# Fused attention layer: bodies of 1024 tokens, values in the score banks after the scores, and the rounding of x on ScalarE

## What is computed

```python
q = _split_heads(jnp.einsum('bfe,ed->bfd', x, W_query))
k = _split_heads(jnp.einsum('bfe,ed->bfd', x, W_key))
v = _split_heads(jnp.einsum('bfe,ed->bfd', x, W_value))
scores = jnp.einsum('hbqd,hbkd->hbqk', q, k)
attn = jax.nn.softmax(scores, axis=-1)
out = jnp.einsum('hbqk,hbkd->hbqd', attn, v)
out = out.transpose(1, 2, 0, 3).reshape(x.shape[0], x.shape[1], HEADS * ATT_D)
out = out + jnp.einsum('bfe,ed->bfd', x, W_res)
return jax.nn.relu(out)
```

## Time and profile before

| what | value |
|---|---|
| median of three runs | 1513.44 us |
| time of the profiled execution | 1513.46 us |
| its span in the trace | 1511.7 us |
| TensorE matmuls, weight loads | busy 1493.1 us, 1405.2 us |
| VectorE, ScalarE, GpSimd | busy 1390.5 us, 1044.5 us, 872.2 us |
| first scores of body 0 start at | 13.71 us |
| value product of the last body starts at | 1504.65 us |
| first projection starts at | 9.71 us |
| transpose of x on VectorE (L349), mean | 701 ns |
| POOL copies of the values (L167), mean | 467 ns |
| DMA | 67.37 MB read, 67.11 MB written, 89 GB/s |

### The profile page before, as it was taken

One profiled execution on the slowest core, in us unless ns is written; L12 is line 12 of the kernel. 1 busy time (PEld: TensorE's weight loads), 2 busy tenths in 40 slices (PEclk: granted clock), 3 DMA queues, 4 the chain that ended last, 5 costly groups with the idle time before them and its releaser, 6 DMA issues.

```text
span 1511.7 us, 77248 instructions
## 1 busy us (share of the span) xinstructions
PE 1493.1 (99%) x32768; PEld 1405.2 (93%) x32768; DVE 1390.5 (92%) x1793; ACT 1044.5 (69%) x1794; POOL 872.2 (58%) x1548
## 2 busy tenths in 40 slices
PE   7999999999999999999999999999999999999997
PEld 6999999999999999999999999999999999999997
DVE  6999999999999999999999999999999999999996
ACT  4677777777777777777777777777777777777775
POOL 3555555555555555555555555555555555555555
PEclk9999999999999999999999999999999999999999
DMA  3444444444444444444444444444444444444443
GB/s 59 98 85 96 85 96 86 96 86 95 86 96 85 96 85 96 85 96 85 96 86 96 86 96 85 96 86 95 86 96 85 96 85 96 85 96 85 96 86 77
DMA packets 677302, 135.36 MB, mean 90 GB/s; under 512 B 545888, under 2 KB 677216, under 8 KB 677216
## 3 DMA queue, kind: packets, MB, share of 16 engines
q1 hardware_dynamic: 675840, 134.30, 42.9%
q10 hardware_dynamic: 1376, 0.26, 0.1%
HBM read 67.37 MB, written 67.11 MB: 89 GB/s over the span
## 4 chain that ended last, share of the span: by engine, by line
PE 98%; issue 0%; POOL 0%; DVE 0%; ACTq 0%; DMA 0%; ACT 0%; POOLq 0%
PE ps_so L241 18%; PE ps_pt L232 17%; PE ps_so L220 14%; PE ps_qk L198 8%; PE ps_qk L196 8%; PE ps_vr L209 8%; PE ps_qk L197 8%; PE ps_vr L210 8%; PE ps_vr L211 8%; POOL y L154 0%; DMA w_raw<-in_L_rec_W_res_dram 0%; ACTq L334 0%; POOL v_diag L167 0%; DVE row_max L364 0%; ACTq L331 0%
## 5 line engine op out<-in xcount | busy, mean ns | idle before, releaser
L154 POOL TENSOR_TENSOR y<-attn,vr 128x256 f32<-128x256 f32 x512 | 387.4, 779 | 532.4 <-DVE attn L379 512.7
L167 POOL COPY v_diag<-vr 64x264 f32<-64x264 f32 x1024 | 478.7, 467 | 102.9 <-POOL y L154 39.9
L311 ACT ACTIVATE probs_t<-ps_pt 128x512 f32<-128x512 f32 x512 | 307.0, 600 | 160.2 <-PE ps_pt L232 160.1
L364 DVE TENSOR_REDUCE row_max<-ps_so 128x16 f32<-128x1024 f32 x256 | 313.5, 1225 | 69.7 <-PE ps_so L220 69.7
L298 ACT COPY vr<-ps_vr 128x512 f32<-128x512 f32 x512 | 300.6, 587 | 67.3 <-PE ps_vr L211 1.1
L196 PE MATMUL ps_qk<-x_hi,w_hi 128*128 128x256 f32 x1024 | 331.3, 323 | 10.5 <-DVE x_lo L355 9.7
L291 ACT COPY qk<-ps_qk 128x512 f32<-128x512 f32 x512 | 300.6, 587 | 56.6 <-PE ps_qk L198 9.0
L232 PE MATMUL ps_pt<-ident,shifted 128*128 128x128 f32 x2048 | 321.4, 280 | 0.8 <-ACT probs_t L311 0.8
L369 DVE TENSOR_TENSOR shifted<-ps_so,row_max 128x1024 f32<-128x1024 f32 x256 | 313.5, 1224 | 8.8
L241 PE MATMUL ps_so<-v_diag,probs_t 128*64 128x66 f32 x8192 | 296.2, 225 | 1.4 <-DVE attn L379 0.7
L198 PE MATMUL ps_qk<-x_lo,w_hi 128*128 128x256 f32 x1024 | 292.0, 285 | 0.0
(11 more groups left out here) (20 smaller groups left out, 1527.2 us busy)
## 6 DMA issues: line engine op xcount, KB each, us to landing
x_in<-in_r_x_dram SPq DMA_DIRECT2D x1024, 64.0 KB, 2.2
out_dram<-y SPq DMA_DIRECT2D x256, 256.0 KB, 2.5
w_raw<-in_L_rec_W_query_dram ACTq DMA_DIRECT2D x1, 64.0 KB, 2.2
w_raw<-in_L_rec_W_key_dram ACTq DMA_DIRECT2D x1, 64.0 KB, 2.7
w_raw<-in_L_rec_W_value_dram ACTq DMA_DIRECT2D x2, 32.0 KB, 2.7
w_raw<-in_L_rec_W_res_dram ACTq DMA_DIRECT2D x2, 32.0 KB, 2.7
```

The lines of the kernel that those rows point to most:

```text
L154: nc.gpsimd.tensor_tensor(y[:, n % 2, a * HALF:(a + 1) * HALF].rearrange("k t (p j d) -> k j (t p) d", j=2, d=D), attn[:, n % 2, a * HALF: ...
L167: nc.gpsimd.tensor_copy(v_diag[n % 2][j * F:(j + 1) * F, seq, :, :, :, j].rearrange("k a t p d -> k a (t p) d"), vr[n][seq * F:(seq + 1) * ...
L364: nc.vector.reduce_max(row_max[:, :].rearrange("q (h u) -> q h u", h=HEADS), scores, AX_X).then_inc(max_ready, 1)
```

## The change

A body becomes 8 tiles, 1024 tokens, so there are 128 bodies. A group is a pair of tiles; a body has four groups (`GROUPS`), and `upto(i, g)` counts them. What the code does differently:

- The scores of a whole body fill the four `ps_so` banks completely (8 tiles of 64 columns) in one run of 64 matmuls. When VectorE has read them, the value product of body i-1 is written into the same banks from column 0 on, in one run of 32 matmuls. There is one body less in flight.
- The bank that is freed goes to a second bank for transposes (`ps_pt[a % 2]`).
- Queries and keys are made with matmuls of 512 columns, 3 in a group, one weight and half the tokens of a body in each group.
- ScalarE rounds x (`round_x`) instead of VectorE; VectorE keeps the transpose and the rest.
- GpSimd moves the values in two halves around the addition of the residual.

```diff
-TILES = 4
+TILES = 8
 HALF = 2
+GROUPS = TILES // HALF
...
-        ps_qk, ps_vr, ps_pt = banks("ps_qk"), banks("ps_vr"), banks("ps_pt")
+        ps_qk, ps_vr = banks("ps_qk"), banks("ps_vr")
+        ps_pt = [banks(f"ps_pt{n}") for n in range(2)]
...
-                if has(i - 3):
-                    sp.wait_ge(y_ready, i - 2)
-                    sp.dma_start(out_bodies[i - 3], y[:, (n + 1) % 2]).then_inc(y_stored[(n + 1) % 2], 16)
+                if has(i - 2):
+                    sp.wait_ge(y_ready, i - 1)
+                    sp.dma_start(out_bodies[i - 2], y[:, n % 2]).then_inc(y_stored[n % 2], 16)
...
             def step(i, n):
...
+                if has(i):
+                    move_values(i, n, 0)
+                if has(i - 1):
+                    add_residual(i - 1, (n + 3) % RING)
+                if has(i):
+                    move_values(i, n, 1)
...
-            def project_qk(i, n, a):
+            def project_qk(i, n, m, g):
                 pe.wait_ge(xlo_ready, i + 1)
-                if a == 1 or has(i - 1):
-                    pe.wait_ge(qk_ready, halves(i, a) - 1)
...
+                if m + g > 0 or has(i - 1):
+                    pe.wait_ge(qk_ready, upto(i, m * 2 + g) - 1)
+                tok = slice(g * QTOK, (g + 1) * QTOK)
+                nc.tensor.matmul(ps_qk[:, :], w_hi[:, m, :], x_hi[n][:, tok], start=True, stop=False)
+                nc.tensor.matmul(ps_qk[:, :], w_lo[:, m, :], x_hi[n][:, tok], start=False, stop=False)
+                nc.tensor.matmul(ps_qk[:, :], w_hi[:, m, :], x_lo[n][:, tok], start=False,
+                                 stop=True).then_inc(qk_done, 1)
...
             def step(i, n):
                 if has(i):
+                    if has(i - 2):
+                        pe.wait_ge(attn_ready, i - 1)
                     if has(i - 1):
                         pe.wait_ge(shifted_ready, i)
...
+                    pe.wait_ge(qk_ready, upto(i, 3))
+                    score(i)
...
+                if has(i - 1):
                     transpose_shifted(i - 1, n + 1, 0)
                 if has(i + 1):
-                    project_qk(i + 1, (n + 1) % RING, 0)
+                    project_qk(i + 1, (n + 1) % RING, 0, 0)
+                if has(i - 1):
+                    transpose_shifted(i - 1, n + 1, 1)
                 if has(i):
                     project_vr(i, n, 0)
...
                 if has(i):
                     project_vr(i, n, 1)
+                if has(i + 1):
+                    project_qk(i + 1, (n + 1) % RING, 1, 0)
+                if has(i - 1):
+                    pe.wait_ge(v_moved, (i - 1) * 8 + 8)
+                    if has(i):
+                        pe.wait_ge(shifted_ready, i + 1)
+                    pe.wait_ge(pt_ready, upto(i - 1, 3))
+                    weigh_values(i - 1, n + 1)
+                if has(i + 1):
+                    project_qk(i + 1, (n + 1) % RING, 1, 1)
+                if has(i):
+                    project_vr(i, n, 2)
+                    project_vr(i, n, 3)
...
+            def round_x(i, n):
+                act.wait_ge(xt_done, i + 1)
+                if has(i - 4):
+                    act.wait_ge(vr_done, upto(i - 4, 3))
+                nc.scalar.copy(x_hi[n][:, :], x_t[:, :]).then_inc(xhi_ready, 1)
...
+                if has(i - 2):
+                    clip(i - 2, n)
+                if has(i + 2):
+                    round_x(i + 2, (n + 2) % RING)
+                if has(i + 1):
+                    copy_qk(i + 1, 1, 1)
+                if has(i):
+                    copy_vr(i, n, 2)
+                    copy_vr(i, n, 3)
...
-                nc.vector.tensor_copy(x_hi[n][:, :], x_t[:, :]).then_inc(xhi_ready, 1)
...
+            def step(i, n):
+                if has(i):
+                    shift_scores(i, n)
                 if has(i + 2):
-                    split_x(i + 2, (n + 2) % RING)
+                    transpose_x(i + 2, (n + 2) % RING)
+                if has(i - 1):
+                    normalize(i - 1, n + 1)
+                if has(i + 2):
+                    rest_of_x(i + 2, (n + 2) % RING)
```

More of the change, by code:

```diff
@@ L97, in run @@
         def run(step):
-            for i in range(N + 3):
+            for i in range(N + 2):
                 step(i, i % RING)
@@ new lines, in move_values @@
+            def move_values(i, n, b):
+                groups = slice(b * GROUPS // 2, (b + 1) * GROUPS // 2)
+                pool.wait_ge(vr_ready, upto(i, b * 2 + 1))
+                if has(i - 2):
+                    pool.wait_ge(o_done, i - 1)
+                if b == 1 and has(i - 1):
+                    pool.wait_ge(sum_ready, halves(i - 1, 1))
+                for j in range(2):
+                    for m, seq in enumerate((1 - j, j)):
+                        nc.gpsimd.tensor_copy(
+                            v_diag[n % 2][j * F:(j + 1) * F, seq, groups, :, :, j].rearrange("k a t p d -> k (a t p) d"),
+                            vr[n][seq * F:(seq + 1) * F, j, groups].rearrange("k a t p d -> k (a t p) d"),
+                        ).then_inc(v_moved, 1)
+                        if m == 0 or j == 1:
+                            pool.wait_ge(v_moved, i * 8 + b * 4 + j * 2 + m + 1)
@@ L188, in _ @@
         def _(pe):
-            def project_qk(i, n, a):
+            def project_qk(i, n, m, g):
                 pe.wait_ge(xlo_ready, i + 1)
-                if a == 1 or has(i - 1):
-                    pe.wait_ge(qk_ready, halves(i, a) - 1)
[L193 to L199, removed]
+                if m + g > 0 or has(i - 1):
[5 more added lines that the diff above has]
+                                 stop=True).then_inc(qk_done, 1)
             def project_vr(i, n, a):
-                if a == 1 or has(i - 1):
-                    pe.wait_ge(vr_ready, halves(i, a) - 1)
+                if a > 0 or has(i - 1):
+                    pe.wait_ge(vr_ready, upto(i, a) - 1)
                 w_vr_hi = w_hi[:, 2:4, :].rearrange("p w c -> p (w c)")
@@ L338, in _ @@
             act.wait_ge(ones_ready, 1)
-            copy_qk(0, 0)
-            copy_qk(0, 1)
+            for i in range(2):
+                round_x(i, i)
+            for m in range(2):
+                for g in range(2):
+                    copy_qk(0, m, g)
             run(step)
@@ L388, in _ @@
                                     ALU.subtract).then_inc(wlo_ready, 1)
-            split_x(0, 0)
-            split_x(1, 1)
+            for i in range(2):
+                transpose_x(i, i)
+                rest_of_x(i, i)
             run(step)
```

190 lines of the change are left out of this document (87 added, 103 removed).

## The result

The changed kernel takes 1834.01 us (median of 4 runs, 1830.36 to 1839.04) against 1513.29 us before. The ratio is 1.2122, with a 95% interval of 1.2089 to 1.2156: 21% slower. I had forecast 1604 us, 6% slower, with a range up to 1642. The direction was right, the size was off by a factor of more than three, and the time lies far outside the range.

The account below looks back on a forecast made before the run. TensorE's list was taken as the bound: 11.30 us of work plus a 0.94 wait gave 12.24 per step. 21.2 + 11.8 + 1554.5 - 1.0 + 15.7 = 1602 us of span, so 1604 us, range 1578 to 1642.

Parts of the forecast that it names:

- TensorE's list is the bound: Whole kernel: TensorE, matmuls covering 99% of the span, bounds it; only shortening its list helps, any wait there hurts.
- The new step, 11.30 us of work: TensorE's work per step if nothing waits: 11.30 us against 11.63 for 1024 tokens, a gain of 0.33.
- The new wait, +0.94 us: Each step, `ps_vr`: group 3 waits for ScalarE's copy of group 2, +0.83, plus 0.11 for an uncovered weight load.
- VectorE is not the bound, taking the rounding off it is worth nothing: VectorE in each step: its work fits before the next maximum, due at 14.1 us, so moving the rounding gains nothing.
- ScalarE is on time: ScalarE in each step: clip and rounding end by 9.5 to 9.9 us, before group 3's copy is wanted at 10.0.
- The ends: Start and end of the kernel: first scores near 21.2 us, step 0 of 11.8 us, a tail of 15.7 us.
- Then 127 steps of 12.24 are 1554.5: Steady part: 127 equal steps of 12.24 us each, 1554.5 us of the forecast span.
- None of the four: Rivals: ScalarE late too (0.07), VectorE and TensorE alternating (0.03), cheaper wide matmuls (0.04), wait mostly hidden (0.04).
- rival 2: Four shared banks: VectorE and TensorE alternate in a strict ring that bounds the step; 1640 to 1670 us, chance 0.03.
- Rival 3: Queries/keys projections: wide matmuls much cheaper, at 0.131 us a step of 11.17 us, about 1467 us; chance 0.04.
- the outer bound: Total time: lowest value from the forecast's own bounds per step, at the outside 1567 to 1648 us.

Follow-up runs that it names:

- experiment 4: Changed kernel with TensorE's steps written out without a loop, and group 2 of values and residual moved ahead of the value product: 1599.56 us.
- experiment 6: Changed kernel without TensorE's loop, queries and keys group 3 put between groups 2 and 3 of values and residual: 1569.72 us, ratio 1.0376.
- experiment 8: Changed kernel without TensorE's loop, rounding of x given back to VectorE between its transpose and its reciprocal: 1621.50 us, ratio 1.0716.
- experiment 9: Changed kernel with three steps instead of four in TensorE's loop body (1497 instructions), buffers in rings of three: 1601.45 us, ratio 1.0582.
- experiment 1: Changed kernel with TensorE's 130 steps written out one behind the other, no loop: 1624.98 us, ratio 1.0718.
- 10: Changed kernel with a loop of three steps and queries and keys group 3 between groups 2 and 3 of values and residual: 1512.53 us, ratio 0.9991.

## Why the prediction was wrong, point by point

- **TensorE's list is the bound.** Right for the steps of the change. They are TensorE's list plus the one wait that was forecast; only in experiment 4 does the path over VectorE's normalisation add 0.3 us.
- **The new step, 11.30 us of work.** 12.22 less the 0.94 for the wait leaves 11.28, but that it came so close is luck. The scores in one run take 1.52 us (939.88 to 941.40) where I had 1.69, and the value product in one run 2.02 where I had 2.16: 0.31 us cheaper. The four groups of queries and keys take 0.78, 0.78, 0.79 and 0.80 us where I had 0.66, 0.66, 0.75 and 0.76: 0.32 us dearer, mostly because the first wide matmul behind transposes lasts 0.32 us until the next starts, and I had priced it like the others. The two misses cancel.
- **The new wait, +0.94 us.** Right: 128 times, 0.96 us from start to start, and TensorE's list of waits shows 86.4 us. The forecast bracket of 0.83 us, 106 us in all, mixed two measures: the bracket counts from the end of the last matmul's record, 0.28 us after its start, and is 0.68 us; the cost counts from the 0.12 us at which the next could have started, and is 0.83. Experiments 4 and 6 took the wait away in part; the step fell by 0.51 and 0.70 us.
- **VectorE is not the bound, taking the rounding off it is worth nothing.** Right, experiment 8. The rounding of 1024 elements takes it 0.69 us.
- **ScalarE is on time.** Right. It copies group 2 at 905.43, 0.32 us after the start of its last matmul. Clip and rounding of double width take 1.06 and 1.04 us.
- **The ends.** The first scores were forecast for 21.2 us and came at 21.78, those of step 1 for 33.0 and came at 33.59. The four first groups took 2.4 us each instead of 2.2. From the last scores to the end I had 11.2 + 15.7 = 26.9 us; experiment 9, which has no stalls, shows 25.5.
- **"Then 127 steps of 12.24 are 1554.5."** This is the step that failed. It took every step as equal, and so put the fetching of TensorE's instructions at nothing without a reason. The change doubled the work in a step and left four steps in a turn of the loop, so its code grew from 1053 to 1993 instructions. I had read the order of the instructions and counted their times, but never their number between the two ends of the loop. 29 jumps of 8.0 us are 232 us. Experiment 9, with the same order of work and a body that is kept, gives 1601.45 us where I had said 1604, by the cancelling misses above and the shorter end.
- **The rivals and the range.** None of the four was it. Of rival 2, the ring of TensorE and VectorE over the four banks, no run shows the whole; its second half bounds experiment 4 at 11.71 us. Rival 3 is refuted by the 0.23 us of a wide matmul. The range was made of prices of instructions and waits alone, so it could not hold a cost of the code. Its sum has a slip as well: twelve matmuls that are 0.01 us cheaper are 0.12 us a step and not 0.08, so the outer bound would be 1562 and not 1567.

Some things stay open. Between 1497 and 1993 instructions I have no size at which the stall begins. And the stalls of the written-out programs cost 24 us in experiment 1 and 57 us in experiment 6 (against 9 and 10); they come at fairly equal distances, but no run shows what sets the distance.

## What to carry to other kernels

When a change makes the body of a loop larger, count the instructions of each engine between the loop's two ends, not only their times, and compare with the largest body that a trace shows to run without a gap behind the jump (here 1497 instructions). A wait for "issue" at equal distances together with much traffic in the queue of instructions is the mark of a program that is fetched again; fewer steps in a turn cured it here, and a hint or writing out the steps did only in part. And two groups that share one bank want about a copy's length of other work between them (the copy is 0.58 us here; three wide matmuls, 0.7 us, took most of the wait away), but the place for that work has to be chosen so that it does not push back a chain that runs over other engines.

## What the hardware showed that I had not expected

- A stall of some 3.5 us costs more than itself: the granted clock fell from 1.00 to 0.50 during it and came back about 10 us later, and the jumps cost 8.0 us each, with 5.3 us of them idle.
- With the hint for the jump the first wait went, but the second grew from 1.5 to about 2.5 us.
- A written-out program is not free of fetch stalls either: up to 1.9 us at a time in experiment 1 and up to 2.9 in experiment 6, about every 14 to 16 steps, with 4 MB of code going through.
- VectorE's `x_lo`, 1.05 us for 512 elements beside GpSimd's additions before, takes 1.21 us for 1024 elements now. In the change it starts just ahead of the addition (905.37 and 905.58 us). Of GpSimd's two additions of 512 elements the first, beside `x_lo`, takes 2.04 us and the second, mostly behind it, 1.18; at the end of the program, where `x_lo` no longer runs, both together take 2.3. It looks as if the one that comes second pays; no experiment was made on it.
